# Edge attributes split by ScalarE and VectorE, VectorE's order laid round msg_lo, and the messages' remainder taken half by VectorE and half by GpSimd

## The chip, the cores and the metric

The kernel runs on one core of a Trainium2 chip. The metric is the device time in microseconds (us) of one execution.

## What is computed

A graph layer (1250 nodes, 20000 edges sorted by their destination, 512 features) is followed by a small mixture of experts. The change lies in the edge stage of the graph layer:

```python
def mish(x):
    return x * jnp.tanh(jax.nn.softplus(x))
src, dst = (edge_index[0], edge_index[1])
edge_feat = jnp.concatenate([x[src], x[dst], edge_attr], axis=-1)
h = mish(edge_feat @ W1 + b1)
messages = mish(h @ W2 + b2)
agg = jax.ops.segment_sum(messages, dst, num_segments=x.shape[0])
...
x = x + _L0_gnn_ref(_layernorm(x, axis=-1), edge_index, edge_attr_64, ...)
x = x + _L0_ffn_ref(_layernorm(x, axis=-1)[None], ...)[0]
```

x[src] @ W1 and x[dst] @ W1 are computed once per node ahead of the stage and stand in two tables in HBM (src_table, dst_table), so that a pair's first layer is two gathers and the product with its 64 edge attributes.

## The kernel before, in words

edge_phase is written out by hand for five engines, each with its own instruction stream and semaphores between them; no scheduler moves anything. The edges are cut into tiles of 128, each of which belongs to one block of 125 destination nodes, and tiles go two by two: 83 pairs (PAIRS). Each engine's stream is a loop over steps s, and in each step it works on several pairs at once, each in another stage. Products are kept near fp32 by splitting an operand into a high part in fp32r and a remainder (hi and lo), and multiplying hi by hi, hi by lo and lo by hi.

In step s:

- **SyncE** (SP) loads indices (idx_sl, L682) and attributes (ea_sl, L683) of pair s+5 into one of four slots.
- **GpSimd** (POOL) issues two indirect DMAs that add dst_table rows into gath for pair s+2 (L696) and two that gather src_table rows for pair s+3 (L706). It then splits the attributes of pair s+2 into ea_hl (L713, L715), and at last takes the remainder msg_lo = act - msg_hi of the messages of pair s-3 (L721), 128x1024 elements.
- **ScalarE** (ACT) computes mish by Exp, Square, Ln, Exp: for the first layer of pair s (exp1 L738, sq1 L746, ln1 L752, quot1 L763) and, alternating with it, for the second layer of pair s-2 (exp2 L743, sq2 L749, ln2 L760, quot2 L766). Between ln1 and ln2 it copies the transposed attributes of pair s+1 out of PSUM (eaT, L757), which waits for TensorE's transposes of the same step.
- **VectorE** (DVE) does the rest of mish: inc1 and inc2 (L782, L785), the products h (L809) and msg (L818), and the casts hTh (L814) and msg_hi (L800). It also adds the segment sums of pair s-4 from PSUM into agg (L793, twice), takes hTl, the remainder of h of pair s-1 (L795), builds the one-hot matrix of pair s-3 (onehot, L802) and the local destinations of pair s+2 (dloc, L806, 128x2 elements).
- **TensorE** (PE) starts with the segment sums of pair s-4 (L842, L843: onehot times msg_hi and msg_lo, two tiles). Then come the second layer's hi tiles of pair s-1 (hTh with W2h and W2l and a bias, L831 and L828, 18 matmuls), the two attribute transposes of pair s+1 (L859), the lo tiles (hTl with W2h, 8 matmuls), eight transposes of gath (L873) and the eight matmuls of eaT with Wch and Wcl (L877, L878), whose end is the semaphore lin1_ps of pair s+1.

Two waits matter in what follows. The segment sums of TensorE's step s wait for onehot, msg_lo and h of pair s-1; the hi tiles wait for msg and hTh of VectorE's step s-1:

```python
pe.wait_ge(S["onehot_ready"], m + 1)
pe.wait_ge(S["msg_lo_ready"], m + 1)
pe.wait_ge(S["h_ready"], min(s, PAIRS))
...
if r >= 2:
    pe.wait_ge(S["msg_ready"], r - 1)
pe.wait_ge(S["h_hi"], r + 1)
```

Here m is s-4 and r is s-1. VectorE makes onehot of pair m in its own step m+3, which is TensorE's step s less one.

## Time and profile before

| | us |
|---|---|
| median of 3 runs | 1414.67 (1414.13 to 1416.09) |
| profiled execution, its own time | 1416.24 |
| its span | 1414.6 |
| PE busy | 1145.5 (81%) |
| PE weight loads busy | 912.1 (64%) |
| DVE busy | 1108.9 (78%) |
| ACT busy | 852.9 (60%) |
| POOL busy | 913.7 (65%) |

The mean granted TensorE clock is 0.933 of full speed. The edge stage runs from about 106 to 1053 us of the span; a node stage and the experts follow. Busy shares over the whole span mix these stages, so the edge stage has to be read by itself: one of its steps repeats every 10.6 us. In the rows, a start and a duration stand ahead of the engine, and the next instruction of an engine often starts up to 0.1 us before the end of the one ahead of it; so what an instruction costs in a chain is its start to the next one's start. A bracket is idle time ahead of an instruction, and what ended it.

### The profile page before, as it was taken

The page shows a single profiled execution, that of the slowest core. Times are in us where ns is not written, and L with a number is a line of the kernel's source. Part 1 is how long each engine was busy: PE and PEld are TensorE (multiplying, and loading weights), DVE is VectorE, ACT ScalarE, POOL GpSimd, SP SyncE. Part 2 cuts the span into 40 slices and gives each one's busy share as a digit, 9 for nine tenths or more (in the row PEclk, how much of TensorE's full clock was granted, in tenths as well). Part 3 has the DMA queues.
Part 4 walks back from the last instruction along what each step waited for, and adds up shares of the span by engine and source line. Part 5 has one row for each costly group of instructions (what it writes and reads, how often), then busy time and mean ns, then how long its engine had stood idle before and what let it go on. Part 6 is the DMA issues. An engine that isn't in the chain of part 4 may idle for free. (4 is left out here: it accounts for less than half of the span.)

```text
span 1414.6 us, 20672 instructions
## 1 busy us (share of the span) xinstructions
PE 1145.5 (81%) x5823; PEld 912.1 (64%) x5824; DVE 1108.9 (78%) x1627; ACT 852.9 (60%) x1061; POOL 913.7 (65%) x755
## 2 busy tenths in 40 slices
PE   0992888889889899899898889889838997559972
PEld 0671666777677677677677777767626775558861
DVE  3840579999999999999999999999864876743364
ACT  1311667777777777777777777777843543333341
POOL 1333788898888888889889889888431210454410
PEclk9996899999999999999999999999968997679965
DMA  5534554554554554455455455455210111634452
GB/s 145 200 116 98 117 107 96 109 114 96 107 111 101 102 111 106 98 111 110 98 109 112 96 110 113 96 106 108 81 38 23 37 44 44 189 106 131 127 164 101
DMA packets 113398, 148.00 MB, mean 105 GB/s; under 512 B 55389, under 2 KB 63980, under 8 KB 113225
## 3 DMA queue, kind: packets, MB, share of 16 engines
q0 software_dynamic: 40912, 101.69, 32.8%
q1 hardware_dynamic: 72377, 45.20, 11.6%
q8 instruction: 41, 0.67, 0.2%
q14 instruction: 52, 0.43, 0.1%
q10 hardware_dynamic: 16, 0.02, 0.0%
HBM read 136.29 MB, written 15.66 MB: 107 GB/s over the span
## 5 line engine op out<-in xcount | busy, mean ns | idle before, releaser
L696 POOL DMA_INDIRECT gath<-dst_table,idx_sl x166 | 283.8, 1709 | 49.7 <-issue 27.2
L828 PE MATMUL ps<-W2l,hTh 128*128 128x512 f32 x664 | 264.2, 398 | 0.0
L828 PE MATMUL ps<-W2h,hTh 128*128 128x512 f32 x664 | 263.5, 397 | 0.0
L721 POOL TENSOR_TENSOR msg_lo<-act,msg_hi 128x1024 fp32r<-128x1024 f32 x83 | 213.3, 2570 | 33.9 <-DVE msg_hi L800 33.9
L706 POOL DMA_INDIRECT gath<-src_table,idx_sl x166 | 171.6, 1034 | 76.7 <-issue 50.3
L806 DVE TENSOR_TENSOR dloc<-idx_sl,block_off 128x2 f32<-128x2 int32 x83 | 180.3, 2172 | 14.9 <-DMA idx_sl<-idx_scr 14.9
L828 PE MATMUL ps<-W2h,hTl 128*128 128x512 f32 x664 | 174.9, 405 | 0.4 <-DVE hTl L795 0.2
L828 PEld LDWEIGHTS ps<-W2l,hTh 128*128 128x128 f32 x664 | 125.7, 189 | 30.6
L828 PEld LDWEIGHTS ps<-W2h,hTh 128*128 128x128 f32 x664 | 126.0, 190 | 26.4
L793 DVE TENSOR_TENSOR agg<-agg,ps 125x512 f32 x166 | 112.9, 680 | 31.0 <-DVE agg L793 23.3
L746 ACT ACTIVATE act<-act 128x1024 f32<-128x1024 f32 x83 | 88.2, 1062 | 77.6 <-DVE act L782 77.6
L828 PEld LDWEIGHTS ps<-W2h,hTl 128*128 128x128 f32 x664 | 118.6, 188 | 24.1 <-DVE hTl L795 1.3
L831 PE MATMUL ps<-bias_r,minus_r 128*128 128x512 f32 x166 | 74.6, 449 | 59.5 <-DVE act L818 59.5
L809 DVE SCALAR_TENSOR_TENSOR act<-act,ps 128x1024 f32<-128x1024 f32 x83 | 100.3, 1208 | 24.8 <-ACT act L763 24.8
L842 PE MATMUL ps<-msg_hi,onehot 128*126 128x512 f32 x166 | 73.2, 441 | 48.5 <-DVE act L809 30.7
L738 ACT ACTIVATE act<-ps 128x1024 f32<-128x1024 f32 x83 | 85.3, 1028 | 39.3 <-PE ps L878 39.3
L818 DVE SCALAR_TENSOR_TENSOR act<-act,ps 128x1024 f32<-128x1024 f32 x83 | 101.4, 1221 | 3.1 <-ACT act L766 0.4
L795 DVE TENSOR_TENSOR hTl<-act,hTh 128x1024 fp32r<-128x1024 f32 x83 | 102.6, 1236 | 0.0
L757 ACT ACTIVATE eaT<-ps 128x256 fp32r<-128x256 f32 x83 | 32.1, 386 | 108.9 <-PE ps L859 108.9
L760 ACT ACTIVATE act<-act,half_col 128x1024 f32<-128x1024 f32 x83 | 94.8, 1143 | 0.1
L831 PEld LDWEIGHTS ps<-bias_r,minus_r 128*128 128x128 f32 x166 | 31.5, 190 | 98.0 <-DVE act L818 94.0
L752 ACT ACTIVATE act<-act,half_col 128x1024 f32<-128x1024 f32 x83 | 94.3, 1137 | 0.1
(315 smaller groups left out, 2852.2 us busy)
## 6 DMA issues: line engine op xcount, KB each, us to landing
f_w_raw<-in_L_ffn_w_dram SPq DMA_DIRECT2D x32, 512.0 KB, 4.6
ea_sl<-ea_scr SPq DMA_DIRECT2D x166, 32.0 KB
ea_scr<-in_edge_attr_dram POOLq DMA_DIRECT2D x1, 5000.0 KB, 20.6
w_raw<-in_L_gnn_W_dram SPq DMA_DIRECT2D x3, 1024.0 KB, 18.6
idx_sl<-idx_scr SPq DMA_DIRECT2D x166, 1.5 KB, 1.7
gath<-src_table,idx_sl POOLq DMA_INDIRECT x166, 4.2
gath<-dst_table,idx_sl POOLq DMA_INDIRECT x166, 5.2
x_raw<-in_x_dram SPq DMA_DIRECT2D x5, 500.0 KB
```

The source lines that it names most:

```text
L696: pool.indirect_dma_start(out=gath[:, k, j, :], out_offset=None, in_=dst_table[:, :], in_offset=bass.IndirectOffsetOnAxis(ap=idx_sl[:, b % ...
L706: pool.indirect_dma_start(out=gath[:, k, j, :], out_offset=None, in_=src_table[:, :], in_offset=bass.IndirectOffsetOnAxis(ap=idx_sl[:, g % ...
L721: nc.gpsimd.tensor_tensor(msg_lo[:, m % 2], act2[:, m % 3], f32(msg_hi[:, m % 2]), ALU.subtract).then_inc(S["msg_lo_ready"], 1)
L752: nc.scalar.activation(a1, a1, ACT.Ln, bias=half_col[:], scale=0.5).then_inc(S["ln1"], 1)
L760: nc.scalar.activation(a2, a2, ACT.Ln, bias=half_col[:], scale=0.5).then_inc(S["ln2"], 1)
L793: nc.vector.tensor_tensor(row, row, two_banks((a + 1) % 2)[0:NB, j, :], ALU.add).then_inc(S["summed"], 1)
L795: nc.vector.tensor_tensor(hTl[:, r % 2], act1[:, r % 2], f32(hTh[:, r % 2]), ALU.subtract).then_inc(S["h_lo"], 1)
L806: nc.vector.tensor_tensor(dloc[:, 2 * n:2 * n + 2], idx_sl[:, n % IN, :, 2], block_off[:, 2 * n:2 * n + 2], ALU.subtract).then_inc(S["dst_ ...
L809: nc.vector.scalar_tensor_tensor(out=act1[:, q % 2], in0=act1[:, q % 2], scalar=1.0, in1=ps_1[:, q % 2], op0=ALU.subtract, op1=ALU.mult).t ...
L818: nc.vector.scalar_tensor_tensor(out=act2[:, g % 3], in0=act2[:, g % 3], scalar=1.0, in1=ps_2[:, g % 2], op0=ALU.subtract, op1=ALU.mult).t ...
L828: return nc.tensor.matmul(ps_2[:, r % 2, j, :], part[:, r % 2, d, j * P:(j + 1) * P], weights[:, d, :], start=False, stop=last)
L831: nc.tensor.matmul(ps_2[:, r % 2, j, :], minus_r[:], bias_r[:, 1, :], start=True, stop=False)
```

## The change

GpSimd no longer splits the attributes. The loads write them twice side by side (ea_sl is 128 columns wide, one more DMA per tile), TensorE transposes that, ScalarE copies all 128 rows as the high part, and VectorE subtracts it in the lower 64 rows (eaT_lo, 64x256 elements). TensorE transposes the attributes between its two lo tiles instead of ahead of both, and the first-layer matmuls wait for eaT_lo. ScalarE's copy stands behind ln2. The remainder of the messages is split: VectorE takes tile 0 right behind msg_hi, GpSimd tile 1 at the head of its step, ahead of the gathers. VectorE's order is new: hTl, msg_hi, msg_lo of tile 0, the two additions to agg, eaT_lo, h, hTh, msg, dloc, onehot.

```diff
@@ -625,8 +625,7 @@
...
         idx_sl = sb("idx_sl", [P, IN, 2, 3], I32)
-        ea_sl = sb("ea_sl", [P, IN, 2, EDIM])
-        ea_hl = sb("ea_hl", [P, 2, 2, 2 * EDIM], F32R)
+        ea_sl = sb("ea_sl", [P, IN, 2, 2 * EDIM])
         eaT = sb("eaT", [2 * EDIM, 2, E2], F32R)
@@ -646,8 +645,8 @@
...
         src_gath, both_gath = slots("src_gath", GA), slots("both_gath", GA)
-        names = ("ea_hi split dst_ready eaT_ps eaT_ready gath_read lin1_ps exp1 inc1 sq1 ln1 quot1 h_ready h_hi h_lo lin2_ps "
-                 "exp2 inc2 sq2 ln2 quot2 msg_ready msg_hi_ready msg_lo_ready onehot_ready sum_ps summed w3_in w3_hi w3_lo").split()
+        names = ("dst_ready eaT_ps eaT_hi eaT_lo gath_read lin1_ps exp1 inc1 sq1 ln1 quot1 h_ready h_hi h_lo lin2_ps "
+                 "exp2 inc2 sq2 ln2 quot2 msg_ready msg_hi_ready msg_lo0_ready msg_lo1_ready onehot_ready sum_ps summed w3_in w3_hi w3_lo").split()
         S = {n: sem("e_" + n) for n in names}
@@ -675,12 +674,13 @@
...
                         sp.wait_ge(*loaded(both_gath, GA, q - IN, 32))
-                        sp.wait_ge(S["split"], q - IN + 1)
+                        sp.wait_ge(S["eaT_ps"], q - IN + 1)
                         sp.wait_ge(S["dst_ready"], q - IN + 1)
...
                         sp.dma_start(idx_sl[:, k, j, :], idx_scr[bass.ds(first, P), :]).then_inc(idx_in[k], 16)
-                        sp.dma_start(ea_sl[:, k, j, :], ea_scr[bass.ds(first, P), :]).then_inc(ea_in[k], 16)
+                        for half in range(2):
+                            sp.dma_start(ea_sl[:, k, j, half * EDIM:(half + 1) * EDIM], ea_scr[bass.ds(first, P), :]).then_inc(ea_in[k], 16)
                 if s == PAIRS - 3:
@@ -688,6 +688,12 @@
...
             for s in range(FIRST, LAST + 1):
+                m = s - 3
+                if exists(m):
+                    pool.wait_ge(S["msg_hi_ready"], m + 1)
+                    if m >= 2:
+                        pool.wait_ge(S["sum_ps"], m - 1)
+                    nc.gpsimd.tensor_tensor(msg_lo[:, m % 2, 1, :], act2[:, m % 3, 1, :], f32(msg_hi[:, m % 2, 1, :]), ALU.subtract).then_inc(S["msg_lo1_ready"], 1)
                 b = s + 2
@@ -705,20 +711,6 @@
...
                                                 in_offset=bass.IndirectOffsetOnAxis(ap=idx_sl[:, g % IN, j, 0:1], axis=0)).then_inc(src_gath[k], 16)
-                if exists(b):
-                    k = b % 2
-                    pool.wait_ge(*loaded(ea_in, IN, b, 32))
-                    if b >= 2:
-                        pool.wait_ge(S["eaT_ps"], b - 1)
-                    nc.gpsimd.tensor_copy(ea_hl[:, k, :, 0:EDIM], ea_sl[:, b % IN]).then_inc(S["ea_hi"], 1)
-                    pool.wait_ge(S["ea_hi"], b + 1)
-                    nc.gpsimd.tensor_tensor(ea_hl[:, k, :, EDIM:2 * EDIM], ea_sl[:, b % IN], f32(ea_hl[:, k, :, 0:EDIM]), ALU.subtract).then_inc(S["split"], 1)
-                m = s - 3
-                if exists(m):
-                    pool.wait_ge(S["msg_hi_ready"], m + 1)
-                    if m >= 2:
-                        pool.wait_ge(S["sum_ps"], m - 1)
-                    nc.gpsimd.tensor_tensor(msg_lo[:, m % 2], act2[:, m % 3], f32(msg_hi[:, m % 2]), ALU.subtract).then_inc(S["msg_lo_ready"], 1)
                 for w in pool_parts.get(s, ()):
@@ -739,7 +731,8 @@
...
                     if g >= 3:
-                        act.wait_ge(S["msg_lo_ready"], g - 2)
+                        act.wait_ge(S["msg_lo0_ready"], g - 2)
+                        act.wait_ge(S["msg_lo1_ready"], g - 2)
                     nc.scalar.activation(a2, ps_2[:, g % 2], ACT.Exp, scale=-1.0).then_inc(S["exp2"], 1)
@@ -750,14 +743,14 @@
...
                     nc.scalar.activation(a1, a1, ACT.Ln, bias=half_col[:], scale=0.5).then_inc(S["ln1"], 1)
+                if second:
+                    act.wait_ge(S["sq2"], g + 1)
+                    nc.scalar.activation(a2, a2, ACT.Ln, bias=half_col[:], scale=0.5).then_inc(S["ln2"], 1)
                 if exists(n):
...
                         act.wait_ge(S["lin1_ps"], n - 1)
-                    nc.scalar.activation(eaT[:, n % 2, :], ps_1[:, n % 2, 0, :], ACT.Copy).then_inc(S["eaT_ready"], 1)
-                if second:
-                    act.wait_ge(S["sq2"], g + 1)
-                    nc.scalar.activation(a2, a2, ACT.Ln, bias=half_col[:], scale=0.5).then_inc(S["ln2"], 1)
+                    nc.scalar.activation(eaT[:, n % 2, :], ps_1[:, n % 2, 0, :], ACT.Copy).then_inc(S["eaT_hi"], 1)
                 if first:
@@ -783,6 +776,15 @@
...
                     nc.vector.tensor_scalar(act2[:, g % 3], act2[:, g % 3], EXP_MAX, 1.0, ALU.min, ALU.add).then_inc(S["inc2"], 1)
+                if exists(r):
+                    nc.vector.tensor_tensor(hTl[:, r % 2], act1[:, r % 2], f32(hTh[:, r % 2]), ALU.subtract).then_inc(S["h_lo"], 1)
+                if exists(m):
+                    if m >= 2:
+                        dve.wait_ge(S["sum_ps"], m - 1)
+                    dve.wait_ge(S["msg_ready"], m + 1)
+                    nc.vector.tensor_copy(msg_hi[:, m % 2], act2[:, m % 3]).then_inc(S["msg_hi_ready"], 1)
+                    dve.wait_ge(S["msg_hi_ready"], m + 1)
+                    nc.vector.tensor_tensor(msg_lo[:, m % 2, 0, :], act2[:, m % 3, 0, :], f32(msg_hi[:, m % 2, 0, :]), ALU.subtract).then_inc(S["msg_lo0_ready"], 1)
                 if exists(a):
@@ -791,19 +793,10 @@
...
                         nc.vector.tensor_tensor(row, row, two_banks((a + 1) % 2)[0:NB, j, :], ALU.add).then_inc(S["summed"], 1)
-                if exists(r):
-                    nc.vector.tensor_tensor(hTl[:, r % 2], act1[:, r % 2], f32(hTh[:, r % 2]), ALU.subtract).then_inc(S["h_lo"], 1)
-                if exists(m):
-                    if m >= 2:
-                        dve.wait_ge(S["sum_ps"], m - 1)
-                    dve.wait_ge(S["msg_ready"], m + 1)
-                    nc.vector.tensor_copy(msg_hi[:, m % 2], act2[:, m % 3]).then_inc(S["msg_hi_ready"], 1)
-                    dve.wait_ge(S["dst_ready"], m + 1)
-                    nc.vector.tensor_tensor(onehot[:, m % 2], iota_n[:].unsqueeze(1).to_broadcast([P, 2, NE]),
-                                            dloc[:, 2 * m:2 * m + 2].unsqueeze(2).to_broadcast([P, 2, NE]), ALU.is_equal).then_inc(S["onehot_ready"], 1)
-                if exists(n):
-                    dve.wait_ge(*loaded(idx_in, IN, n, 32))
-                    nc.vector.tensor_tensor(dloc[:, 2 * n:2 * n + 2], idx_sl[:, n % IN, :, 2], block_off[:, 2 * n:2 * n + 2], ALU.subtract).then_inc(S["dst_ready"], 1)
+                t = s + 1
+                if exists(t):
+                    dve.wait_ge(S["eaT_hi"], t + 1)
+                    nc.vector.tensor_tensor(eaT[EDIM:, t % 2, :], ps_1[EDIM:, t % 2, 0, :], f32(eaT[EDIM:, t % 2, :]), ALU.subtract).then_inc(S["eaT_lo"], 1)
                 if exists(q):
@@ -817,6 +810,13 @@
...
                                                    op0=ALU.subtract, op1=ALU.mult).then_inc(S["msg_ready"], 1)
+                if exists(n):
+                    dve.wait_ge(*loaded(idx_in, IN, n, 32))
+                    nc.vector.tensor_tensor(dloc[:, 2 * n:2 * n + 2], idx_sl[:, n % IN, :, 2], block_off[:, 2 * n:2 * n + 2], ALU.subtract).then_inc(S["dst_ready"], 1)
+                if exists(m):
+                    dve.wait_ge(S["dst_ready"], m + 1)
+                    nc.vector.tensor_tensor(onehot[:, m % 2], iota_n[:].unsqueeze(1).to_broadcast([P, 2, NE]),
+                                            dloc[:, 2 * m:2 * m + 2].unsqueeze(2).to_broadcast([P, 2, NE]), ALU.is_equal).then_inc(S["onehot_ready"], 1)
                 lo_parts(s)
@@ -836,7 +836,8 @@
...
                     pe.wait_ge(S["onehot_ready"], m + 1)
-                    pe.wait_ge(S["msg_lo_ready"], m + 1)
+                    pe.wait_ge(S["msg_lo0_ready"], m + 1)
+                    pe.wait_ge(S["msg_lo1_ready"], m + 1)
                     pe.wait_ge(S["h_ready"], min(s, PAIRS))
@@ -848,27 +849,34 @@
...
                     hi_tile(1)
+                def lo_tile(j):
+                    for d in range(KC):
+                        ins = lin2(j, d, hTl, W2h, d == KC - 1)
+                    return ins
+
+                if exists(r):
+                    pe.wait_ge(S["h_lo"], r + 1)
+                    lo_tile(0)
                 if exists(n):
                     k = n % 2
-                    pe.wait_ge(S["split"], n + 1)
+                    pe.wait_ge(*loaded(ea_in, IN, n, 64))
                     if n >= 2:
...
                     if n >= 5:
-                        pe.wait_ge(S["summed"], (n - 4) * 2)
+                        pe.wait_ge(S["summed"], (n - 5) * 2 + 1)
                     for j in range(2):
-                        ins = nc.tensor.transpose(ps_1[:, k, 0, j * P:(j + 1) * P], f32(ea_hl[:, k, j, :]), ident[:])
+                        ins = nc.tensor.transpose(ps_1[:, k, 0, j * P:(j + 1) * P], ea_sl[:, n % IN, j, :], ident[:])
                     ins.then_inc(S["eaT_ps"], 1)
                 if exists(r):
-                    pe.wait_ge(S["h_lo"], r + 1)
-                    for j in range(2):
-                        for d in range(KC):
-                            ins = lin2(j, d, hTl, W2h, d == KC - 1)
-                    ins.then_inc(S["lin2_ps"], 1)
+                    lo_tile(1).then_inc(S["lin2_ps"], 1)
                 if exists(n):
                     k = n % 2
-                    pe.wait_ge(S["eaT_ready"], n + 1)
                     pe.wait_ge(*loaded(both_gath, GA, n, 32))
-                    for d in range(KC):
+                    if n >= 5:
+                        pe.wait_ge(S["summed"], (n - 4) * 2)
+                    for d in (2, 3, 0, 1):
+                        if d == 0:
+                            pe.wait_ge(S["eaT_lo"], n + 1)
                         for j in range(2):
```

VectorE, one step in the middle of the edge stage, before, from hTl to the first instruction of the next step (L809 is h, L814 hTh, L818 msg, L782 inc1):

```order
L795 TENSOR_TENSOR hTl<-act,hTh 128x1024
L800 CAST msg_hi<-act 128x1024
L802 TENSOR_TENSOR onehot<-iota_n,dloc 128x252
L806 TENSOR_TENSOR dloc<-idx_sl,block_off 128x2
L809 SCALAR_TENSOR_TENSOR act<-act,ps 128x1024
L814 CAST hTh<-act 128x1024
L818 SCALAR_TENSOR_TENSOR act<-act,ps 128x1024
L782 TENSOR_SCALAR act<-act 128x1024
```

There onehot and dloc stand between msg_hi and h, and msg ends the step. VectorE now, one step from msg_hi on (L787 is msg_lo of tile 0, L799 eaT_lo, L802 h, L811 msg, L775 inc1 of the next step):

```order
L785 CAST msg_hi<-act 128x1024
L787 TENSOR_TENSOR msg_lo<-act,msg_hi 128x512
L790 TENSOR_LOAD block_i
L790 ISA x2
L795 ISA
L795 TENSOR_TENSOR agg<-agg,ps 125x512
```

```order
L799 TENSOR_TENSOR eaT<-ps,eaT 64x256
L802 SCALAR_TENSOR_TENSOR act<-act,ps 128x1024
L807 CAST hTh<-act 128x1024
L811 SCALAR_TENSOR_TENSOR act<-act,ps 128x1024
L815 TENSOR_TENSOR dloc<-idx_sl,block_off 128x2
L818 TENSOR_TENSOR onehot<-iota_n,dloc 128x252
L775 TENSOR_SCALAR act<-act 128x1024
```

dloc and onehot have moved behind msg, to the end of the step. TensorE now, from the last hi matmul of a step to the first of the next (L828 with hTl are the lo tiles, L868 the attribute transposes, L843 and L844 the segment sums):

```order
L828 MATMUL ps<-W2l,hTh 128x512
L828 MATMUL ps<-W2h,hTl 128x512 x4
L868 MATMUL ps<-ident,ea_sl 128x128 x2
L828 MATMUL ps<-W2h,hTl 128x512 x4
L881 MATMUL ps<-ident,gath 128x128 x8
L885 MATMUL ps<-eaT,Wch 128x256
L886 MATMUL ps<-eaT,Wcl 128x256
```

```order
L843 MATMUL ps<-msg_hi,onehot 126x512
L844 MATMUL ps<-msg_lo,onehot 126x512
L843 MATMUL ps<-msg_hi,onehot 126x512
L844 MATMUL ps<-msg_lo,onehot 126x512
L831 MATMUL ps<-bias_r,minus_r 128x512
```

The attribute transposes stand four matmuls later than before, and the segment sums are still the first thing of a step, ahead of the hi tiles.

## Rows read from the trace of the kernel before

**Rows 1.** Windows view, 202 to 992 us: busy PE, PEld, DVE, ACT, POOL; clock; DMA

```profile
202.00:992.00 790.00, 705.29 (x3550) 558.54 (x3549) 763.52 (x815) 614.36 (x666) 703.45 (x519) 1.00 0.52 106
```

**Rows 2.** Timeline of VectorE; start us, us, engine line op out<-in count [idle before <-releaser]

```profile
606.30 2.36 DVE L806 TENSOR_TENSOR dloc<-idx_sl,block_off 128x2 f32<-128x2 int32 x1
608.58 1.21 DVE L809 SCALAR_TENSOR_TENSOR act<-act,ps 128x1024 f32<-128x1024 f32 x1
609.82 0.69 DVE L814 CAST hTh<-act 128x1024 fp32r<-128x1024 f32 x1
610.55 1.22 DVE L818 SCALAR_TENSOR_TENSOR act<-act,ps 128x1024 f32<-128x1024 f32 x1
611.69 0.75 DVE L782 TENSOR_SCALAR act<-act 128x1024 f32<-128x1024 f32 x1
```

**Rows 3.** Timeline of GpSimd, the same stretch

```profile
606.06 2.58 POOL L721 TENSOR_TENSOR msg_lo<-act,msg_hi 128x1024 fp32r<-128x1024 f32 x1
```

**Rows 4.** Tile views of dloc, onehot and agg: ns min/median/max, first and last start

```profile
L806 DVE TENSOR_TENSOR dloc<-idx_sl,block_off x83: 145/2356/2368, 118.0 to 1000.4; 128x2 f32<-128x2 int32 x83
L802 DVE TENSOR_TENSOR onehot<-iota_n,dloc x83: 407/672/682, 168.0 to 1043.1; 128x252 fp32r<-128x252 f32 x83
...
L793 DVE TENSOR_TENSOR agg<-agg,ps x166: 667/687/690, 183.0 to 1048.9; 125x512 f32 x166
```

**Rows 5.** Timeline of TensorE, one step

```profile
601.25 0.50 PE L831 MATMUL ps<-bias_r,minus_r 128*128 128x512 f32 x1 [0.72 <-DVE act L818]
...
605.54 0.38 PE L859 MATMUL ps<-ident,ea_hl 128*128 128x128 f32 x2
605.68 2.11 PE L828 MATMUL ps<-W2h,hTl 128*128 128x512 f32 x8
607.62 1.03 PE L873 MATMUL ps<-ident,gath 128*128 128x128 f32 x8
...
609.33 0.28 PE L878 MATMUL ps<-eaT,Wcl 128*128 128x256 f32 x1
609.93 0.47 PE L842 MATMUL ps<-msg_hi,onehot 128*126 128x512 f32 x1 [0.33 <-DVE act L809]
...
610.70 0.39 PE L843 MATMUL ps<-msg_lo,onehot 128*126 128x512 f32 x1
611.82 0.50 PE L831 MATMUL ps<-bias_r,minus_r 128*128 128x512 f32 x1 [0.74 <-DVE act L818]
```

**Rows 6.** Timeline of ScalarE, the same step

```profile
605.96 0.39 ACT L757 ACTIVATE eaT<-ps 128x256 fp32r<-128x256 f32 x1 [1.02 <-PE ps L859]
606.24 1.14 ACT L760 ACTIVATE act<-act,half_col 128x1024 f32<-128x1024 f32 x1
607.28 1.05 ACT L763 ACTIVATE act<-act 128x1024 f32<-128x1024 f32 x1
```

**Rows 7.** Windows view, 165 to 170 and 180 to 185 us, columns as in rows 1

```profile
165.00:170.00 5.00, 4.86 (x14) 3.85 (x15) 3.79 (x7) 3.15 (x4) 3.06 (x4) 0.66 0.70 163
180.00:185.00 5.00, 4.21 (x10) 3.38 (x11) 1.20 (x2) 0.70 (x1) 4.23 (x4) 0.50 0.40 63
```

**Rows 8.** Timeline of TensorE, first matmul of the hi tiles, steps 5 and 81

```profile
194.49 0.50 PE L831 MATMUL ps<-bias_r,minus_r 128*128 128x512 f32 x1 [0.74 <-DVE act L818]
...
1006.03 0.50 PE L831 MATMUL ps<-bias_r,minus_r 128*128 128x512 f32 x1 [0.71 <-DVE act L818]
```

**Rows 9.** Timeline of TensorE, gaps while the stage fills

```profile
159.01 0.44 PE L859 MATMUL ps<-ident,ea_hl 128*128 128x128 f32 x2 [1.55 <-POOL ea_hl L715]
...
165.15 0.51 PE L831 MATMUL ps<-bias_r,minus_r 128*128 128x512 f32 x1 [2.01 <-DVE act L818]
...
165.76 0.63 PE L828 MATMUL ps<-W2l,hTh 128*128 128x512 f32 x1
...
169.14 0.39 PE L828 MATMUL ps<-W2h,hTh 128*128 128x512 f32 x1
...
180.79 0.76 PE L842 MATMUL ps<-msg_hi,onehot 128*126 128x512 f32 x1 [5.72 <-POOL msg_lo L721]
```


## The prediction

> **What bounds the kernel now.** I read the windows view first, then the timelines of one step of the edge stage engine by engine, then the tile views, and last the timelines of its start and end.
>
> The windows view of the steady edge stage [rows 1] shows the TensorE clock at full grant (2.4 GHz) and VectorE busy for 763.5 of 790 us, with TensorE and GpSimd at 89% each. The stage decides: from the first matmul of step 5's hi tiles to that of step 81 [rows 8] 811.5 us pass, 76 steps, 10.68 us each. The step of the timeline has 10.57 us (601.25 to 611.82) [rows 5]; the rest is a few longer steps.
>
> Full engines are not yet a bound, so I ask which wait ends last. VectorE's dloc, a subtraction of 128x2 elements, has 2.36 us in the timeline and 0.145 us at its shortest [rows 2, 4]. It ends at 608.66, and GpSimd's msg_lo, started at 606.06, ends at 608.64 [rows 3]. So dloc stands still until GpSimd's subtraction is over; 2.2 of VectorE's 10.3 us per step (763.5 us over 74 steps) are this. The Trainium skill, SBUF — State Buffer, section "SBUF: two separate sides", says that a GpSimd instruction and a VectorE one with two SBUF inputs exclude each other for a whole instruction, whichever starts first. By that rule, the trace agrees.
>
> Beside it lies a closed chain through four engines, and it is nearly as long. From the first matmul of the hi tiles: 18 matmuls to the attribute transposes, 4.29 us (601.25 to 605.54); 0.42 until ScalarE starts the copy eaT, which had waited 1.02 us for it; 0.28 to ln2; 1.04 to quot1; quot1 itself 1.05; 0.04 to VectorE (what TensorE's end to ScalarE's start takes: 605.92 to 605.96); h to hTh 1.24, hTh to msg 0.73, msg 1.22, and 0.05 to the next hi tiles [rows 2, 5, 6]. That makes 10.36 us, against 10.57: only 0.2 us of slack. The segment sums cost this chain nothing before, because they wait for h only and run while VectorE does hTh and msg (609.93 to 611.1) [rows 5].
>
> **What the change does to that chain.** A step of TensorE begins with the segment sums, and these need onehot, which VectorE now makes as the last thing of its step. So the chain is now closed over onehot and the segment sums. Beginning at the first segment matmul, with the durations of the rows:
>
> - segment sums, four matmuls: 0.77 for three spacings and 0.23 for the fourth, 1.00. Formerly hidden, now in the chain.
> - hi tiles, 18 matmuls: 4.20. Their 4.29 contain some 0.1 that a first matmul after a wait takes longer (0.50 against 0.39 us), and they wait no more.
> - lo tile 0, now ahead of the transposes: half of 605.68 to 607.62, 0.97. Added.
> - transposes until ScalarE starts: 0.42 as before. The operand is ea_sl and as large.
> - copy eaT to quot1: 0.28. ln2 stands ahead of the copy now, which takes its 1.04 out of the chain.
> - quot1 1.05, to VectorE 0.04, h 1.24, hTh 0.73, msg to the next instruction 1.14.
> - dloc: between 0.1 (its shortest 0.145, with the usual overlap) and 2.36, if GpSimd's subtraction still ran. That starts right behind msg_hi, many microseconds earlier, so I take 0.10.
> - onehot: 0.41 at its shortest, 0.67 at its median [rows 4], where it overlapped GpSimd's work. Same reason, 0.41.
> - to TensorE: 0.14, as from the end of h at 609.79 to the first segment matmul at 609.93 [rows 2, 5].
>
> The sum is 1.00 + 4.20 + 0.97 + 0.42 + 0.28 + 1.05 + 0.04 + 1.24 + 0.73 + 1.14 + 0.10 + 0.41 + 0.14 = **11.72 us per step**, 1.04 more than the mean of 10.68. It is a floor: each link waits for the one ahead, whatever the engines have spare.
>
> **The parts that lie beside it.** VectorE loses 2.2 us of standing still and 0.26 of onehot's stretching, and gains msg_lo of tile 0 (0.69, as the 125x512 addition to agg) and eaT_lo (0.41 as onehot, which has as many elements): 9.0 us per step of 11.7. Both additions lie ahead of h, where VectorE waits for quot1. Should GpSimd's half of msg_lo start first, VectorE's half stands still for half of 2.58, 1.3 us, and 2.7 us of waiting cover that. If GpSimd comes second, it only finishes later. If these 2.7 us were gone, h would be late, and the chain with it. eaT_lo can start when the copy has ended, 0.39 after its start, and ends some 0.85 after it, ahead of quot1's end; TensorE needs it after lo tile 1 and four gath transposes, about as late, so 0, at most 0.2. GpSimd sheds the attribute split and half of msg_lo, and was at 9.5 of 10.68; its gathers now queue behind the wait for msg_hi, but it needs about 8 us of 11.7, and each gather has over a step until TensorE reads it. SyncE issues two more DMAs per step, and waits for TensorE's transposes where it waited for GpSimd's split. The slots are four deep and the DMA engines half idle (0.52) [rows 1]: 0. ScalarE's work is the same.
>
> **TensorE's clock.** TensorE's own work in a step is 1.00 + 4.20 and, from the transposes to the end of the last matmul (605.54 to 609.61), 4.07: 9.27 us. With 11.72 us per step it stands idle for 2.45 us in one piece. Before, its gaps were 0.33 and 0.74 us, and the grant stayed at 1.00 [rows 1, 5]. While the stage filled there were longer ones [rows 9]: after 1.55 us idle the clock held; after 2.01 us, eight matmuls from 165.76 to 169.14 took 3.38 us, where 8 x 0.233 = 1.86 is usual, and the granted clock of that window is 0.66 [rows 7], which is part at 1.2 GHz and part at 2.4. Then it came back, in the midst of the hi tiles. So such a fall costs 1.52 us, in the hi tiles, on the chain. A gap of 2.45 lies beyond the one that was followed by a fall, so I take it for likely in most steps, and charge 0.85 of 1.52, which is my choice: 1.3 us. The bounds are 0 and 1.8 (a fall in every step, longer than that one by a matmul or two). A slower stretch doesn't shorten the gap, since it lengthens work and chain alike.
>
> **The sum.** 11.72 + 1.3 = 13.0 us per step; 76 x 13.0 = 988, less 811.5, is +176.5 us. At the ends: step 4's segment sums waited 5.72 us for msg_lo behind GpSimd's gathers [rows 9], which goes, as msg_lo is at the head of the queue now. With the longer chain in its place I count -4.5, and -1.5 for the first attributes, that no longer wait for GpSimd. The last two or three steps keep onehot behind msg, +3. Together -3. 1416.2 + 176.5 - 3 = 1589.7 for the profiled execution, which was 1.6 above the median of the runs: **1588 us**.
>
> **The rivals.**
>
> *The clock holds.* Then only the chain's 11.72 counts: 76 x 11.72 = 890.7, +79.2, less 3 and 1.6: 1491 us. For it: one gap of 2.01 is thin evidence, and the share of idle time (2.45 of 11.72) is small. Against: the two neighbouring rows, 1.55 held and 2.01 fell, and 2.45 is past both. Chance 0.26.
>
> *The clock stays down throughout.* As at 180 to 185 us, where the grant was 0.50 [rows 7] after a gap of 5.72. Then the TensorE part of the chain (1.00 + 4.20 + 0.97 = 6.17) stretches by 3.38/1.86 = 1.82 to 11.2, the rest is 5.55, and a step 16.8: 76 x 16.8 = 1277, +465, some 1877 us. Against it: at 169.14 the clock came back during the hi tiles, and it would here. Chance 0.04.
>
> *The relief decides (faster).* The place is VectorE's dloc behind GpSimd's msg_lo. If I have misread onehot's place in the chain, so that it or the segment sums were ready early, the chain is 11.72 - 1.00 - 0.10 - 0.41 = 10.2 us, and VectorE (9.0) and GpSimd (8) lie under it. 76 x 10.2 = 775, -36; less 3 and 1.6, 1375 us. It decides from the point where onehot ends before h does. By the lock rule of the Trainium skill (SBUF — State Buffer, "SBUF: two separate sides") alone, the change is a gain, since the exclusion leaves the full engines. For it: VectorE and GpSimd are the fullest. Against: the new order has onehot behind msg, TensorE's has the segment sums ahead of the hi tiles, and no queue can pass its own head. Chance 0.05. Nearly no change, from effects that cancel: 0.02.
>
> **How the numbers follow.** Forecast 1588 us, chance 0.63; its own range 1540 (a fall in half of the steps, 0.75 each, +136) to 1625 (13.5 per step, +214). The range of 8 in 10 takes in the holding clock, 1480 to 1625; below it lies the relief, above it the clock that stays down. Two tenths of a percent, 3 us, is about what a measurement here can tell from no change. Faster 0.05, same 0.02, slower 0.93.
>
> **What would show it.** In the changed kernel's profile: TensorE idle some 2.4 us in one piece ahead of the segment sums, ended by onehot, and none ahead of the hi tiles; the granted clock of the stage below 1.00, about 0.9, with matmuls of 0.63 us in the hi tiles; ScalarE's copy waiting over 2 us for the transposes; dloc at 0.15 and onehot at 0.41 us; VectorE waiting for quot1 ahead of h; GpSimd waiting for msg_hi. If TensorE waits ahead of the segment sums for something other than onehot, or the step is below 11.5 us, the chain is wrong; if the grant is 1.00, the clock's term is.

## The result, and the profile after

| | before | after |
|---|---|---|
| median of the runs | 1414.4 us (4 runs) | 1575.31 us (4 runs, 1573.92 to 1576.97) |
| ratio, 95% interval | | 1.1135 (1.1116 to 1.1155) |
| span of the profiled execution | 1414.6 us | 1575.4 us |
| mean granted TensorE clock | 0.933 | 0.879 |
| DVE busy | 1108.9 us | 1015.8 us |
| POOL busy | 913.7 us | 705.5 us |

The kernel is 11% slower, 1575.3 us where 1588 were forecast, and VectorE and GpSimd have less to do than before. The changed kernel's windows view of the steady edge stage, as [rows 1] (busy PE, PEld, DVE, ACT, POOL; granted clock; DMA share; GB/s):

```profile
202.00:1145.00 943.00, 769.50 (x3524) 625.27 (x3525) 665.23 (x959) 611.36 (x662) 509.81 (x368) 0.90 0.46 93
```

VectorE falls from 763.5 of 790 us to 665 of 943, TensorE from 89% to 82%, and the grant from 1.00 to 0.90. No engine is full now, so what lengthened the step is a wait. The tile view of onehot in the changed kernel (ns min/median/max, first and last start) names it, with who waited for it (us, times):

```profile
L818 DVE TENSOR_TENSOR onehot<-iota_n,dloc x83: 412/414/418, 178.0 to 1205.5; 128x252 fp32r<-128x252 f32 x83
...
who waited for it (us, times):
  PEld ps L843: 214.2, 82
  PE ps L843: 196.5, 82
```

TensorE's segment sums waited for onehot in 82 of 83 pairs, 196.5 us in all. In the kernel before, the gap ahead of the segment sums was 0.33 us and ended by h [rows 5]. Two steps of the changed kernel's TensorE timeline (the hi tiles' other matmuls left out):

```profile
601.90 0.50 PE L843 MATMUL ps<-msg_hi,onehot 128*126 128x512 f32 x1 [2.32 <-DVE onehot L818]
...
602.94 0.57 PE L831 MATMUL ps<-bias_r,minus_r 128*128 128x512 f32 x1
...
606.58 0.39 PE L831 MATMUL ps<-bias_r,minus_r 128*128 128x512 f32 x1
...
609.61 0.38 PE L868 MATMUL ps<-ident,ea_sl 128*128 128x128 f32 x2
...
612.47 0.28 PE L886 MATMUL ps<-eaT,Wcl 128*128 128x256 f32 x1
615.05 0.50 PE L843 MATMUL ps<-msg_hi,onehot 128*126 128x512 f32 x1 [2.31 <-DVE onehot L818]
...
616.09 0.39 PE L831 MATMUL ps<-bias_r,minus_r 128*128 128x512 f32 x1
...
618.18 0.40 PE L831 MATMUL ps<-bias_r,minus_r 128*128 128x512 f32 x1
...
621.21 0.38 PE L868 MATMUL ps<-ident,ea_sl 128*128 128x128 f32 x2
...
626.93 0.79 PE L843 MATMUL ps<-msg_hi,onehot 128*126 128x512 f32 x1 [2.59 <-DVE onehot L818]
```

Each step has one gap of 2.3 to 2.6 us, ended by onehot, and none ahead of the hi tiles. The first step has 13.15 us (601.90 to 615.05), the second 11.88. The nine matmuls of the first hi tile take 3.64 us in the one (602.94 to 606.58) and 2.09 in the other (616.09 to 618.18), 1.55 less. The granted clock is 0.51 from 603.0 to 606.5 us and 1.00 from 616.0 to 620.0: the first tile ran for the most part at the lower of the two clock levels (1.2 GHz). The gap ahead of the two was the same, 2.32 and 2.31 us. Of the first 78 steps from one such gap to the next (three more, at the stage's end, have other work in them), 59 hold matmuls of over 0.6 us and last 13.15 us. The 19 others come in two kinds, 6 of 11.60 us and 13 of 11.88, 11.8 in the mean. In the 13, VectorE's cast hTh has 0.95 to 0.98 us; in the 6 it has 0.69, and in the 59 it is never over 0.72. So a fall of the clock costs 1.55 us, 13.15 less 11.60, the same as the first hi tile shows.

The rest of the chain in the changed kernel's timelines, ScalarE first, then VectorE:

```profile
610.03 0.39 ACT L753 ACTIVATE eaT<-ps 128x256 fp32r<-128x256 f32 x1 [3.46 <-PE ps L868]
610.31 1.05 ACT L756 ACTIVATE act<-act 128x1024 f32<-128x1024 f32 x1
```

```profile
611.39 1.22 DVE L802 SCALAR_TENSOR_TENSOR act<-act,ps 128x1024 f32<-128x1024 f32 x1 [0.52 <-ACT act L756]
612.65 0.69 DVE L807 CAST hTh<-act 128x1024 fp32r<-128x1024 f32 x1
613.38 1.22 DVE L811 SCALAR_TENSOR_TENSOR act<-act,ps 128x1024 f32<-128x1024 f32 x1
614.51 0.15 DVE L815 TENSOR_TENSOR dloc<-idx_sl,block_off 128x2 f32<-128x2 int32 x1
614.59 0.41 DVE L818 TENSOR_TENSOR onehot<-iota_n,dloc 128x252 fp32r<-128x252 f32 x1
```

From the transposes at 609.61: 0.42 to the copy, 0.28 to quot1, 1.08 to h, 1.26, 0.73, 1.13, 0.08, then onehot 0.41 and 0.05 to the segment sums at 615.05. dloc is 0.15 us again, against 2.36 [rows 2].

### The profile page after: what moved, and what is told of

Its sections match the earlier page's. It is cut to its first block and busy times, and to the rows that moved or that the text cites. A ratio compares the mean times of both kernels' runs of the same rounds, so it can differ in the third digit from the quotient of the medians.

```text
span 1575.4 us, 21001 instructions
## 1 busy us (share of the span) xinstructions
PE 1213.5 (77%) x5823; PEld 983.6 (62%) x5824; DVE 1015.8 (64%) x1793; ACT 853.2 (54%) x1061; POOL 705.5 (45%) x589
## 5 line engine op out<-in xcount | busy, mean ns | idle before, releaser
L696 POOL TENSOR_TENSOR msg_lo<-act,msg_hi 128x512 fp32r<-128x512 f32 x83 | 148.2, 1786 | 398.5 <-DVE msg_hi L785 398.5
L828 PE MATMUL ps<-W2h,hTh 128*128 128x512 f32 x664 | 303.4, 457 | 0.0
L828 PE MATMUL ps<-W2l,hTh 128*128 128x512 f32 x664 | 298.0, 449 | 0.0
L843 PE MATMUL ps<-msg_hi,onehot 128*126 128x512 f32 x166 | 84.0, 506 | 196.5 <-DVE onehot L818 196.5
L828 PE MATMUL ps<-W2h,hTl 128*128 128x512 f32 x664 | 186.3, 405 | 0.0
L799 DVE TENSOR_TENSOR eaT<-ps,eaT 64x256 fp32r<-64x256 f32 x83 | 35.5, 428 | 231.0 <-ACT eaT L753 229.0
L828 PEld LDWEIGHTS ps<-W2h,hTh 128*128 128x128 f32 x664 | 152.3, 229 | 39.6
L828 PEld LDWEIGHTS ps<-W2l,hTh 128*128 128x128 f32 x664 | 150.5, 227 | 39.3
L843 PEld LDWEIGHTS ps<-msg_hi,onehot 128*126 128x126 f32 x166 | 33.9, 204 | 218.8 <-DVE onehot L818 214.2
L828 PEld LDWEIGHTS ps<-W2h,hTl 128*128 128x128 f32 x664 | 118.6, 188 | 22.9
L802 DVE SCALAR_TENSOR_TENSOR act<-act,ps 128x1024 f32<-128x1024 f32 x83 | 101.4, 1221 | 42.4 <-ACT act L756 21.7
L811 DVE SCALAR_TENSOR_TENSOR act<-act,ps 128x1024 f32<-128x1024 f32 x83 | 101.4, 1221 | 3.1 <-ACT act L759 0.3
L881 PE MATMUL ps<-ident,gath 128*128 128x128 f32 x664 | 87.9, 276 | 17.2 <-DMA gath<-dst_table,idx_sl 17.2
L881 PEld LDWEIGHTS ps<-ident,gath 128*128 128x128 f32 x664 | 78.7, 142 | 29.0 <-DMA gath<-dst_table,idx_sl 18.2
L748 ACT ACTIVATE act<-act,half_col 128x1024 f32<-128x1024 f32 x83 | 94.3, 1137 | 0.1
```

Source lines behind the costliest of these rows:

```text
L696: nc.gpsimd.tensor_tensor(msg_lo[:, m % 2, 1, :], act2[:, m % 3, 1, :], f32(msg_hi[:, m % 2, 1, :]), ALU.subtract).then_inc(S["msg_lo1_rea ...
L748: nc.scalar.activation(a2, a2, ACT.Ln, bias=half_col[:], scale=0.5).then_inc(S["ln2"], 1)
L802: nc.vector.scalar_tensor_tensor(out=act1[:, q % 2], in0=act1[:, q % 2], scalar=1.0, in1=ps_1[:, q % 2], op0=ALU.subtract, op1=ALU.mult).t ...
L811: nc.vector.scalar_tensor_tensor(out=act2[:, g % 3], in0=act2[:, g % 3], scalar=1.0, in1=ps_2[:, g % 2], op0=ALU.subtract, op1=ALU.mult).t ...
L828: return nc.tensor.matmul(ps_2[:, r % 2, j, :], part[:, r % 2, d, j * P:(j + 1) * P], weights[:, d, :], start=False, stop=last)
L843: nc.tensor.matmul(o[0:NE, j, :], onehot[:, m % 2, j, :], msg_hi[:, m % 2, j, :], start=True, stop=False)
```

## The experiments

Theory A is the prediction's: the step is set by a chain that closes over onehot and the segment sums, and by what the clock does in the gap that this opens. In the table, a step is the mean over the same 75 steps of each trace (the 7th to the 81st of the 82 intervals between first Wcl matmuls of the first layer). A ratio is to the kernel before on the same chip, whose medians were 1414.4 (after), 1415.3 (e1 to e4), 1417.0 (e5 to e7) and 1417.5 us (e8).

| kernel | median us | ratio to before, 95% | step, us |
|---|---|---|---|
| before | 1414.4 | | 10.68 |
| after | 1575.3 | 1.1135 (1.1116 to 1.1155) | 12.83 |
| e1, onehot early | 1377.3 | 0.9730 (0.9706 to 0.9754) | 10.32 |
| e2, onehot alone late | 1584.2 | 1.1202 (1.1173 to 1.1231) | 12.84 |
| e3, gap filled | 1495.7 | 1.0576 (1.0551 to 1.0600) | 11.83 |
| e4, transposes early | 1407.7 | 0.9944 (0.9921 to 0.9966) | 10.71 |
| e5, both moved | 1373.7 | 0.9691 (0.9661 to 0.9721) | 10.25 |
| e6, before with dloc free | 1396.8 | 0.9869 (0.9837 to 0.9902) | 10.43 |
| e7, onehot beside GpSimd | 1428.3 | 1.0075 (1.0047 to 1.0103) | 10.96 |
| e8, sums first | 1356.2 | 0.9570 (0.9539 to 0.9601) | 9.98 |

**e1: onehot early.** One part of the change undone, in the changed kernel:

```diff
+                if exists(n):
+                    dve.wait_ge(*loaded(idx_in, IN, n, 32))
+                    nc.vector.tensor_tensor(dloc[:, 2 * n:2 * n + 2], idx_sl[:, n % IN, :, 2], block_off[:, 2 * n:2 * n + 2], ALU.subtract).then_inc(S["dst_ready"], 1)
+                if exists(m):
+                    dve.wait_ge(S["dst_ready"], m + 1)
+                    nc.vector.tensor_tensor(onehot[:, m % 2], iota_n[:].unsqueeze(1).to_broadcast([P, 2, NE]),
...
                 t = s + 1
                 if exists(t):
                     dve.wait_ge(S["eaT_hi"], t + 1)
...
-                if exists(n):
-                    dve.wait_ge(*loaded(idx_in, IN, n, 32))
...
-                if exists(m):
-                    dve.wait_ge(S["dst_ready"], m + 1)
...
                 lo_parts(s)
```

> The changed kernel with dloc and onehot moved from the end of VectorE's step to the place behind the additions to agg, ahead of eaT_lo and h; nothing else. Theory A (the chain over onehot and the segment sums sets the step): the chain is again closed from msg to the hi tiles, 4.29 + 0.97 + 0.42 + 0.28 + 1.05 + 0.04 + 1.24 + 0.73 + 1.22 + 0.05 = 10.3 us per step instead of 12.8, TensorE's gaps are below 1.2 us and its grant is 1.00, so the time is about 1575 - 76 x 2.5 = 1385 us (1375 to 1400). Theory B (the work added to VectorE, the doubled attribute loads and the smaller share of GpSimd cost the time): the time stays above 1480.

1377.3 us and 10.32 us per step, where the chain gave 10.3. With onehot back ahead of h the whole loss is gone; the rest of the change, with its added subtractions and doubled attribute loads, is a gain of 38 us on the kernel before. Two rows of its TensorE timeline show the segment sums back beside hTh and msg, and the first hi matmul waiting for msg as in [rows 5]:

```profile
604.91 0.47 PE L843 MATMUL ps<-msg_hi,onehot 128*126 128x512 f32 x1
...
606.83 0.50 PE L831 MATMUL ps<-bias_r,minus_r 128*128 128x512 f32 x1 [0.76 <-DVE act L818]
```

**e2: onehot alone late.** The same part alone, in the kernel before:

```diff
                     nc.vector.tensor_copy(msg_hi[:, m % 2], act2[:, m % 3]).then_inc(S["msg_hi_ready"], 1)
-                    dve.wait_ge(S["dst_ready"], m + 1)
-                    nc.vector.tensor_tensor(onehot[:, m % 2], iota_n[:].unsqueeze(1).to_broadcast([P, 2, NE]),
...
                                                    op0=ALU.subtract, op1=ALU.mult).then_inc(S["msg_ready"], 1)
+                if exists(m):
+                    dve.wait_ge(S["dst_ready"], m + 1)
+                    nc.vector.tensor_tensor(onehot[:, m % 2], iota_n[:].unsqueeze(1).to_broadcast([P, 2, NE]),
...
```

> The kernel before with one edit: onehot moved from behind msg_hi to the end of VectorE's step. Theory A: chain 1.00 + 4.20 + 0.42 + 0.28 + 1.04 + 1.05 + 0.04 + 1.24 + 0.73 + 1.14 + 0.41 + 0.14 = 11.7 us, a gap of 2.4 us ahead of the segment sums, a fall of the clock in some three steps of four at 1.4 us each, 12.7 to 12.8 us per step, 1565 to 1580 us: this one edit costs what the whole change costs. Theory B: within 20 us of the kernel before, 1414 us.

1584.2 us, 4 above the expected band: this one instruction moved costs 169 us by itself, more than the whole change. Its steps without a fall have 11.64 us in the mean, against 11.7 by the chain. Its gap, and its windows view (columns as before):

```profile
605.17 0.49 PE L843 MATMUL ps<-msg_hi,onehot 128*126 128x512 f32 x1 [2.38 <-DVE onehot L819]
```

```profile
202.00:950.00 748.00, 609.25 (x2803) 495.13 (x2801) 464.54 (x641) 484.88 (x527) 524.56 (x409) 0.90 0.45 88
```

**e3: the gap filled.** The clock's part by itself, in the changed kernel; the added matmuls write where the segment sums write next:

```diff
+                    pe.wait_ge(S["h_ready"], min(s, PAIRS))
+                    for f in range(8):
+                        nc.tensor.matmul(o[:, f % 2, :], Wch[:, 0:P], W2h[:, f % KC, :], start=True, stop=True)
                     pe.wait_ge(S["onehot_ready"], m + 1)
```

> The changed kernel with eight more matmuls (128x128 by 128x512) per step on TensorE, behind the wait for h and ahead of the wait for onehot; the segment sums overwrite what they write. Theory A with the clock: 1.9 us of the gap of 2.4 us are filled, the grant stays at 1.00, every step takes 11.6 to 11.9 us, and the time falls to 1575 - 76 x 1.05 = 1495 us though work was added (1485 to 1510). Rival (steps of 13.15 us have another cause than TensorE's idle gap, such as late gathers): 1575 us or more, with the grant still near 0.90.

1495.7 us: the kernel got 80 us faster by 664 matmuls more. Its steps are 11.6 and 11.9 us, those of the changed kernel that had no slow matmuls, and the grant is 1.00. Its windows view and two gaps, one step apart:

```profile
202.00:950.00 748.00, 715.69 (x3542) 572.80 (x3541) 581.80 (x822) 525.27 (x569) 444.44 (x317) 1.00 0.49 101
```

```profile
601.91 0.50 PE L846 MATMUL ps<-msg_hi,onehot 128*126 128x512 f32 x1 [0.57 <-DVE onehot L818]
...
613.78 0.49 PE L846 MATMUL ps<-msg_hi,onehot 128*126 128x512 f32 x1 [0.58 <-DVE onehot L818]
```

So of the 161 us that the change costs, 80 go with the falls of the clock, and 81 are left for the longer chain, less what the relief gives back. The 59 falls by themselves are 91 us; some 14 of them come back as a longer hTh, which has over 0.9 us in 63 of e3's 83 pairs and in 13 of the changed kernel's.

**e4: transposes early.** In the changed kernel, TensorE's wait for h_lo and lo_tile(0) moved behind the attribute transposes:

```diff
-                if exists(r):
-                    pe.wait_ge(S["h_lo"], r + 1)
-                    lo_tile(0)
                 if exists(n):
                     k = n % 2
                     pe.wait_ge(*loaded(ea_in, IN, n, 64))
...
                 if exists(r):
+                    pe.wait_ge(S["h_lo"], r + 1)
+                    lo_tile(0)
                     lo_tile(1).then_inc(S["lin2_ps"], 1)
```

> The changed kernel with the attribute transposes put back ahead of both lo tiles; onehot stays at the end. Theory A: the chain loses 0.97 us and is 10.8; the gap ahead of the segment sums is 1.5 us, about the 1.55 after which the clock held, so the grant is near 1.00 and the time about 1575 - 76 x 2.0 = 1420 us (1410 to 1440). Rival 1 (the clock falls after 1.5 us too, in three steps of four): 1500 us. Rival 2 (the transposes are not on the chain): 1575 us.

1407.7 us, 2 below the band. The step lost 2.12 us: 1.17 by the clock (59 falls in 78 steps at 1.55 us each), for the gap shrank to 1.4 us and no matmul is slow; 0.89 by the chain (10.71 against 11.60, where lo tile 0 has 0.94 in the changed kernel's timeline); and 0.05 by hTh, which has at most 0.75 us in all but one pair. All 75 steps lie between 10.66 and 10.82. One gap of its TensorE timeline:

```profile
615.50 0.50 PE L843 MATMUL ps<-msg_hi,onehot 128*126 128x512 f32 x1 [1.44 <-DVE onehot L818]
```

With those four lo matmuls left where they were, the change would have been 0.6% faster than the kernel before, late onehot and all. So the late onehot makes the loss only in a chain this long. In e2, where the lo tiles stand behind the transposes, ln2 stands behind the copy and keeps the chain (11.64) and the gap (2.38) as long as the changed kernel's.

**e5: both moved.** The edits of e1 and e4 together; of each the line that moved:

```diff
+                    nc.vector.tensor_tensor(onehot[:, m % 2], iota_n[:].unsqueeze(1).to_broadcast([P, 2, NE]),
...
                 t = s + 1
...
                         ins = nc.tensor.transpose(ps_1[:, k, 0, j * P:(j + 1) * P], ea_sl[:, n % IN, j, :], ident[:])
...
+                    lo_tile(0)
                     lo_tile(1).then_inc(S["lin2_ps"], 1)
```

> e1_onehot_early and e4_transposes_early together: onehot ahead of h, and the attribute transposes ahead of both lo tiles. Theory A: the chain from hi tiles to hi tiles is 4.29 + 0.42 + 0.28 + 1.05 + 0.04 + 1.24 + 0.73 + 1.22 + 0.05 = 9.3 us, but another one, over two steps, comes next: from the hi tiles to the end of the first layer 8.36, from there by exp1, exp2, sq1, sq2, ln1, ln2, the copy and quot1 to h about 7.3, h, hTh and msg to the hi tiles 3.25, 18.9 us for two steps, 9.45 each. So 9.45 to 9.7 us per step and 1377 - 76 x 0.75 = about 1320 us (1310 to 1335). Rival (something that the chains leave out, such as the gathers' latency or the queues, holds the step at 10 us or more): above 1350 us.

1373.7 us and 10.25 per step: a miss by 54 us. The chains left out a wait. TensorE's transposes wait for `summed`, the first addition to agg, since they write into the PSUM bank that held the segment sums. VectorE's first addition and TensorE's transposes, in e5's timelines:

```profile
611.36 0.69 DVE L795 TENSOR_TENSOR agg<-agg,ps 125x512 f32 x1
```

```profile
612.19 0.41 PE L865 MATMUL ps<-ident,ea_sl 128*128 128x128 f32 x2 [0.71 <-DVE agg L795]
```

The addition ends at 612.05, the transposes start at 612.19. The change put both additions behind hTl, msg_hi and msg_lo, and with everything else shortened this closes another chain. By e5's timelines it runs from the transposes (612.19) through the first layer to exp1 (616.33), from there by exp2 to inc2 (618.30), and through hTl, msg_hi and msg_lo to the next first addition (621.59) and the next transposes (622.42): 10.23 us.

**e6: the kernel before with dloc free.** It asks what bounded the kernel before, which the prediction left between GpSimd's queue and the standing still of dloc.

```diff
+                if exists(n):
+                    dve.wait_ge(*loaded(idx_in, IN, n, 32))
+                    nc.vector.tensor_tensor(dloc[:, 2 * n:2 * n + 2], idx_sl[:, n % IN, :, 2], block_off[:, 2 * n:2 * n + 2], ALU.subtract).then_inc(S["dst_ready"], 1)
                 if exists(m):
                     if m >= 2:
                         dve.wait_ge(S["sum_ps"], m - 1)
...
-                if exists(n):
-                    dve.wait_ge(*loaded(idx_in, IN, n, 32))
...
                 if exists(q):
                     dve.wait_ge(S["quot1"], q + 1)
```

> The kernel before with dloc moved ahead of msg_hi, where GpSimd's msg_lo does not run; onehot then stands alone against its start. dloc should fall from 2.36 to 0.15 us. Theory Q (GpSimd's queue is what fills a step of the kernel before: gathers, split and msg_lo follow each other without waits): the 2.2 us of dloc cost nothing, the step stays within 0.1 us of 10.68, the time within 8 us of 1415. Theory L (the standing still of dloc is what sets the step): the step falls to the chain's 10.36 us, 1415 - 76 x 0.3 = 1392 us or less.

1396.8 us: nearer to theory L, 5 above its band. The step of its timeline is 10.37 us, the 10.36 of the chain in the prediction; the mean is 10.43. VectorE now waits 1.84 us for quot1 ahead of h, where dloc had stood still:

```profile
604.42 0.15 DVE L798 TENSOR_TENSOR dloc<-idx_sl,block_off 128x2 f32<-128x2 int32 x1
...
607.44 1.22 DVE L809 SCALAR_TENSOR_TENSOR act<-act,ps 128x1024 f32<-128x1024 f32 x1 [1.84 <-ACT act L763]
```

GpSimd's own subtractions are shorter here too (its msg_lo 2.40 us against 2.58), so its queue was eased as well; the run doesn't part these two.

**e7: onehot beside GpSimd's half.** In e1, dloc and onehot moved two places up, behind VectorE's msg_lo and ahead of the additions to agg:

```diff
+                if exists(n):
+                    dve.wait_ge(*loaded(idx_in, IN, n, 32))
...
+                if exists(m):
+                    dve.wait_ge(S["dst_ready"], m + 1)
...
                 if exists(a):
                     for j in range(2):
...
-                if exists(n):
-                    dve.wait_ge(*loaded(idx_in, IN, n, 32))
...
-                if exists(m):
-                    dve.wait_ge(S["dst_ready"], m + 1)
...
                 t = s + 1
```

> e1_onehot_early with dloc and onehot two places earlier, right behind VectorE's half of msg_lo, while GpSimd's half runs. By the exclusion seen in the kernel before, dloc stands still until GpSimd's half ends, some 1.1 us (1.2 to 1.3 us long instead of 0.15), and everything behind it moves by as much; VectorE has about 1.2 us of waiting left per step in e1, so the step stays at 10.3 to 10.5 us and the time at 1377 to 1390 us. If there is no such exclusion, dloc is 0.15 us long and the time is that of e1.

dloc did what was expected, the time did not. GpSimd's half, VectorE's dloc and TensorE's transposes in e7's timelines:

```profile
609.17 1.79 POOL L696 TENSOR_TENSOR msg_lo<-act,msg_hi 128x512 fp32r<-128x512 f32 x1 [2.92 <-DVE msg_hi L785]
```

```profile
609.74 1.25 DVE L790 TENSOR_TENSOR dloc<-idx_sl,block_off 128x2 f32<-128x2 int32 x1
```

```profile
612.06 0.41 PE L868 MATMUL ps<-ident,ea_sl 128*128 128x128 f32 x2 [0.50 <-DVE agg L802]
```

dloc has 1.25 us and ends with GpSimd's subtraction (610.99 and 610.96): the exclusion is shown again, in another place. But VectorE's waiting lay behind the additions to agg, not ahead of them, and the transposes waited for the additions, so 0.64 of the 1.1 us show in the step (10.96 against 10.32): 1428.3 us, 51 more than e1.

**e8: the sums first.** From e5, with VectorE's additions to agg moved to right behind inc2, and dloc and onehot to behind hTl, ahead of msg_hi:

```diff
+                if exists(a):
+                    for j in range(2):
...
                 if exists(r):
                     nc.vector.tensor_tensor(hTl[:, r % 2], act1[:, r % 2], f32(hTh[:, r % 2]), ALU.subtract).then_inc(S["h_lo"], 1)
+                if exists(n):
+                    dve.wait_ge(*loaded(idx_in, IN, n, 32))
...
+                if exists(m):
+                    if m >= 2:
+                        dve.wait_ge(S["sum_ps"], m - 1)
+                    dve.wait_ge(S["dst_ready"], m + 1)
...
                 if exists(m):
                     if m >= 2:
                         dve.wait_ge(S["sum_ps"], m - 1)
...
-                if exists(a):
-                    for j in range(2):
...
```

> e5_both_moved with VectorE's order inc1, inc2, agg, agg, hTl, dloc, onehot, msg_hi, msg_lo of tile 0, eaT_lo, h. In e5 the attribute transposes waited for the first addition to agg, which stood behind hTl, msg_hi and msg_lo; here it follows inc2, so that chain is 2.5 us shorter. Theory A': the step of e5 (10.24 us) was set by that wait; now the two-step chain of 18.9 us comes next, 9.45 to 9.75 us per step, and the time is 1374 - 76 x 0.65 = about 1325 us (1310 to 1345). Rival (the wait only took the blame, and something such as GpSimd's queue or the gathers holds the step): 1360 us or more.

1356.2 us, between the two expectations, and the fastest of all: 4.3% below the kernel before (ratio 0.957, 0.9539 to 0.9601). TensorE's wait for agg is gone and the step 0.27 us shorter. This run moved dloc and onehot too, and e5 had missed its steps of 9.45 to 9.7 by 0.55 us or more, so what this gives back is half of that miss at most. The step of its timeline from 604.54 to 614.11 has 9.57 us, within the 9.45 to 9.75 expected, but the mean is 9.98. What fills the rest is open. The step behind that one, 10.53 us, shows where the time lies. VectorE's first addition to agg in the two steps, and TensorE's lo tiles in the second:

```profile
605.90 0.69 DVE L786 TENSOR_TENSOR agg<-agg,ps 125x512 f32 x1
616.44 0.69 DVE L786 TENSOR_TENSOR agg<-agg,ps 125x512 f32 x1 [0.81 <-issue]
```

```profile
619.22 2.14 PE L830 MATMUL ps<-W2h,hTl 128*128 128x512 f32 x8 [0.42 <-DVE hTl L788]
```

VectorE's two additions start late, hTl with them, and the lo tiles wait for hTl. In the 77 steps from one wait of the hi tiles to the next, VectorE is idle ahead of the two additions for less than 0.5 us in 33 steps, 9.64 us long in the mean, and for more in 44, of 10.20 us. What holds the additions the profile doesn't say ("issue"). The GpSimd timeline has candidates:

```profile
607.46 2.30 POOL L712 DMA_INDIRECT gath<-src_table,idx_sl  x1 [0.30 <-issue]
609.77 1.74 POOL L696 TENSOR_TENSOR msg_lo<-act,msg_hi 128x512 fp32r<-128x512 f32 x1
612.46 1.78 POOL L702 DMA_INDIRECT gath<-dst_table,idx_sl  x1 [0.94 <-DMA gath<-src_table,idx_sl]
```

One gather issue has 2.30 us where 1.0 is usual, and the next gather waits for the landing of the one before. The 15 steps that hold an issue of over 2.2 us are short, 9.60 us in the mean, and the steps behind them long, 10.46. That these set the longer steps was not tried.

## Why the prediction was right

*The bound of the kernel before.* The chain of 10.36 us was right: freed of dloc's standing still, the kernel before ran steps of 10.37 us (e6). dloc behind GpSimd's msg_lo, together with what its release did for GpSimd's queue, cost 1.3% or some 19 us in all, not 2.2 us per step.

*The chain over onehot.* Forecast 11.72 us; the steps without slow matmuls and with hTh at its 0.69 us have 11.60, those with the longer hTh 11.88, and e3's mean is 11.83. Single terms: msg to dloc 1.13 against 1.14, dloc 0.08 against 0.10, h to hTh 1.26 against 1.24. onehot to TensorE was 0.05, not 0.14. e1 takes onehot out of the chain and e2 puts nothing but onehot into it, and both times follow, so the cause is shown. How much a late onehot costs hangs on the length of the rest: 198 us with lo tile 0 ahead of the transposes (the changed kernel against e1), some 34 with it behind them (e4 against e5).

*The parts beside it.* msg_lo of tile 0 has 0.693 us (0.69 forecast), eaT_lo 0.428 (0.41). GpSimd's half has 1.80 us, 1.30 at its shortest: it starts 0.04 us behind VectorE's half (604.87 and 604.83 in the timelines). VectorE's waiting lies for the most part ahead of eaT_lo, for ScalarE's copy (3.21 us at 610.45), and only 0.52 us of it ahead of h. All of this was covered: e1 has the same parts and keeps the step of its chain.

*The clock.* The gap was forecast at 2.45 us and is 2.30 to 2.60. A fall costs 1.55 us where 1.52 was forecast. 59 of 78 steps, 0.76, hold one, where I chose 0.85; no row gave that share, and that it came within 0.1 was luck. Together 1.17 us per step instead of 1.3. This is the step "charge 0.85 of 1.52", and the share in it is the mis-sized term, some 9 us too many over 76 steps. The chain's floor, 11.72 for 11.60, is another 9, of which the longer hTh in 13 of 78 steps gave back 4. e3 shows that the gap is the cause. The lower end of the forecast's own range was added up wrongly: its +136 gives 1548 us, not 1540.

*The ends.* -3 us forecast. The steps make 76 x (12.83 - 10.68) = 163 us, the spans differ by 161, so -2.

*The relief as a rival.* It was real, 38 us in e1, but could not show while onehot closed the chain. The rule of the Trainium skill, SBUF — State Buffer, section "SBUF: two separate sides", that a GpSimd instruction and a VectorE one with two SBUF inputs exclude each other, was borne out by e7 (dloc 1.25 us beside GpSimd's half), and its release by e6 (0.15 us). Alone it gave the wrong sign for the change: its release in the kernel before is worth some 19 us (e6), and the change lost 161.

## What to carry to other kernels

Before you move an instruction within an engine's order, list who waits for it and what stands first in that engine's next step; a cheap operation (0.41 us) cost 169 us here because its reader stands ahead of the longest block of matmuls. Close every chain through the engines once around the loop and sum it before and after; leave out no wait that guards a buffer, as I did with agg in e5 and e7. And where the new chain leaves TensorE idle in one piece, read in the trace what its clock did after gaps of that length: half of this loss was the clock's.

## What I had not expected

- Steps without a fall come in two lengths, 11.60 and 11.88 us, and hTh's cast alone parts them: 0.97 us instead of 0.69 (624.25 in the changed kernel's VectorE timeline). A gather issue of GpSimd runs beside its start (623.71 to 624.71), and the next begins at 625.01. What lengthened it was not tried.
- The same gap of TensorE (2.32 and 2.31 us) was followed by slow matmuls once and not the next time; after the gaps of e4's steady steps, 1.3 to 1.5 us, they never came.
- GpSimd's issue of a gather stretched from 1.0 to 2.30 us in e8, where VectorE's subtraction hTl, onehot and the cast msg_hi ran beside it.
